# A recurrent feature encoder on one core: first digits ahead, halves of h exchanged by DMA, the wide cell half a round sooner, and a dense layer that reads h in place

## The reference, cut to what matters

```python
def lstm_last(x, Wx, Wh, b):          # x: [B, T, E]
    def step(carry, xt):
        h, c = carry
        i, f, gg, o = jnp.split(xt @ Wx + h @ Wh + b, 4, axis=-1)
        c = sigmoid(f) * c + sigmoid(i) * tanh(gg)
        h = sigmoid(o) * tanh(c)
        return (h, c), None
...
m_from = lstm_last(base_emb[from_seq], seq_Wx, seq_Wh, seq_b)    # T = 64, H = 64
m_to = lstm_last(base_emb[to_seq], seq_Wx, seq_Wh, seq_b)
...
x = concatenate([ne[nums], fe[fr]], axis=-1)                     # 11 features, T = 32, E = 8, H = 8
nwf = vmap(enc)(...)
...
feats = concatenate([goby, is_indel, matches_ref, m_from, m_to, count_fwd, count_rev, nwf], axis=-1)
return relu(feats @ reduce_W + reduce_b)                         # [2048, 64]
```

## Time and profile before

| | |
|---|---|
| median of 3 runs | 1803.08 us (1800.8 to 1803.32) |
| the profiled execution | 1799.57 us |
| its span, first to last instruction | 1797.7 us |
| TensorE (PE) busy | 1680.6 us, 93% |
| VectorE (DVE) busy | 1462.9 us, 81% |
| ScalarE (ACT) busy | 1464.5 us, 81% |
| GpSimd (POOL) busy | 944.8 us, 53% |
| mean granted TensorE clock | 0.987 of full speed |
| read from HBM | 474.17 MB |

### The profile page before, as it was taken

One profiled execution on the slowest core, in us unless ns is written; L12 is line 12 of the kernel. 1 busy time (PEld: TensorE's weight loads), 2 busy tenths in 40 slices (PEclk: granted clock), 3 DMA queues, 4 the chain that ended last, 5 costly groups with the idle time before them and its releaser, 6 DMA issues.

```text
span 1797.7 us, 59515 instructions
## 1 busy us (share of the span) xinstructions
PE 1680.6 (93%) x24900; PEld 765.0 (43%) x24900; DVE 1462.9 (81%) x1443; ACT 1464.5 (81%) x2531; POOL 944.8 (53%) x478
## 2 busy tenths in 40 slices
PE   2789999999999999999999999999999999999995
PEld 0234444444444444444444444444444444444444
DVE  6768888888888888988888888888888888888771
ACT  1468888888888888888888888888888888888883
POOL 5346666666666666444444444444554444444552
PEclk9899999999999999999999999999999999999997
DMA  6868898999988988889898888989888888888832
GB/s 224 299 223 261 281 290 285 275 289 277 293 279 284 286 284 285 276 270 298 277 284 289 275 277 278 290 277 285 280 286 279 282 272 296 283 277 282 282 119 49
DMA packets 153476, 484.37 MB, mean 269 GB/s; under 512 B 39240, under 2 KB 95096, under 8 KB 108024
## 3 DMA queue, kind: packets, MB, share of 16 engines
q1 hardware_dynamic: 149532, 479.52, 82.5%
q0 software_dynamic: 2560, 0.15, 0.5%
q10 hardware_dynamic: 1116, 0.88, 0.1%
HBM read 474.17 MB, written 6.09 MB: 267 GB/s over the span
## 4 chain that ended last, share of the span: by engine, by line
PE 64%; ACT 18%; POOL 7%; issue 6%; DMA 1%; SPq 0%; DVE 0%; ACTq 0%; POOLq 0%
PE ab L515 28%; PE e_ps L438 15%; PE f_ps L515 10%; ACT gate L555 10%; PE ab L465 7%; POOL nwf_h L612 4%; ACT tanh_c L555 4%; POOL ig L585 4%; PE ab L401 3%; ACT seq_x L408 2%; ACT f_ps L564 1%; ACT gate L564 1%; ACT nwf_x L478 1%; DMA last_h<-nwf_h 0%; PE e_ps L828 0%
## 5 line engine op out<-in xcount | busy, mean ns | idle before, releaser
L585 POOL TENSOR_TENSOR ig<-gate 128x1024 f32<-128x1024 f32 x192 | 411.1, 2141 | 810.1 <-ACT seq_x L408 404.2
L428 DVE TENSOR_SCALAR hot<-low,cst 128x4096 bf16<-128x4096 bf16 x352 | 453.4, 1288 | 152.8 <-PE e_ps L438 149.4
L438 PE MATMUL e_ps<-hot,tab 128*32 128x512 bf16 x8448 | 527.2, 384 | 15.9 <-DVE kept L450 15.9
L450 DVE SCALAR_TENSOR_TENSOR kept<-high,cst,e_ps 128x1024 f32<-128x1024 uint8 x352 | 448.8, 1275 | 32.9 <-PE e_ps L438 22.1
L515 PE MATMUL ab<-seq_h,seq_wh 64*64 64x512 f32 x3072 | 411.0, 593 | 0.0
L438 PEld LDWEIGHTS e_ps<-hot,tab 128*32 128x32 bf16 x8448 | 204.3, 97 | 399.0 <-issue 228.9
L612 POOL TENSOR_TENSOR seq_h<-gate,tanh_c 128x1024 f32<-128x1024 f32 x128 | 303.9, 2374 | 1.4 <-ACT tanh_c L555 1.4
L562 ACT ACTIVATE gate<-ab 128x1024 f32<-128x1024 f32 x256 | 263.2, 1028 | 18.2 <-PE ab L515 15.0
L555 ACT ACTIVATE tanh_c<-seq_c 64x512 f32<-64x512 f32 (+1 forms) x384 | 241.9, 630 | 25.3 <-POOL nwf_h L612 22.2
L555 ACT ACTIVATE gate<-ab 64x512 f32<-64x512 f32 (+1 forms) x384 | 228.3, 595 | 11.5
L564 ACT ACTIVATE gate<-ab,nwf_bias 128x256 f32<-128x256 f32 (+1 forms) x384 | 147.4, 456 | 104.0 <-PE ab L515 99.9
(11 more groups left out here) (67 smaller groups left out, 1608.5 us busy)
## 6 DMA issues: line engine op xcount, KB each, us to landing
low<-low_digits SPq DMA_DIRECT2D x352, 1024.0 KB, 8.0
tok<-seq_tokens SPq DMA_DIRECT2D x128, 384.0 KB, 4.9
high<-high_digits SPq DMA_DIRECT2D x1408, 32.0 KB
raw<-in_indices SPq DMA_DIRECT2D x32, 176.0 KB
low_digits<-low_of SPq DMA_DIRECT2D x32, 88.0 KB, 3.0
high_digits<-high_of SPq DMA_DIRECT2D x32, 44.0 KB, 3.6
gate<-in_tokens SPq DMA_DIRECT2D x1, 1024.0 KB, 5.7
low<-last_h SPq DMA_DIRECT2D x11, 64.0 KB
```

What stands on the lines that cost most here:

```text
L428: nc.vector.tensor_scalar(hot[:, p % HOT_RING, :, :, :].rearrange("p g u c -> p (g u c)"), low[:, p % LOW_RING, :, :].rearrange("p u c -> ...
L438: last = nc.tensor.matmul(e_ps[32 * g:32 * g + 32, i, :], tab[:, part, 2 * m + ty, :], hot[:, p % HOT_RING, g, i, :], start=(part == 0), s ...
L450: nc.vector.scalar_tensor_tensor(out=kept[:, p % KEPT_RING, :, :].rearrange("p u c -> p (u c)"), in0=high[:, p % HIGH_RING, :, :].rearrang ...
L585: nc.gpsimd.tensor_tensor(ig[:, cols], gates[0][:, n % 2, cols], gates[1][:, n % 2, cols], ALU.mult).then_inc(ig_ready, 1)
```

## The change

- `CELLS`: the wide nwf cell of step r stands at the end of round r, and the narrow cell of step r - 1 behind the first two seq cells. The list ends with the narrow cell alone.
- The shares of pairs are 2, 2, 1, 2, 2, 2 (in the first round 2, 2, 2, 2, 3).
- nwf gate 3 and tanh of c are made in place (fewer, wider pieces), so block 1 of h has its halves swapped; SP's queue issues two DMAs (`move_q`) for each nwf cell that put them right into a second tile `nwf_hq`, from which the next step's products read block 1. The products and the new h wait for `q_moved`.
- Step 0 of each cell leaves out the product with h, and h is no longer set to zero.
- The start: the indices of round 0 and their digits come first; tokens are loaded, stored and broadcast by the ACT queue; the digits of round 1 are made in cell 0, those of round 2 in cell 3; the few indices in cell 1; the small weights are placed by VectorE in cells 2 and 3; the gathers begin in cell 8. In cells 1 to 4, GpSimd makes the last cell's h ahead of the input product.
- The end: no transfer through DRAM. The weights of the 88 small dimensions are loaded once a row and spread by a mask over four slots (`place_dense_w`), and 44 products of 32 rows by 256 columns read the last h as it lies; four more take the small embeddings.

```diff
-for _r in range(NWF_T + 1):
-    for _p in range(2):
-        if _r < NWF_T:
-            CELLS += [("seq", 2 * _r + _p, 0), ("seq", 2 * _r + _p, 1)]
-        if _r:
-            CELLS.append(("nwf", _r - 1, _p))
+for _r in range(NWF_T):
+    CELLS += [("seq", 2 * _r, 0), ("seq", 2 * _r, 1)]
+    if _r:
+        CELLS.append(("nwf", _r - 1, 1))
+    CELLS += [("seq", 2 * _r + 1, 0), ("seq", 2 * _r + 1, 1), ("nwf", _r, 0)]
+CELLS.append(("nwf", NWF_T - 1, 1))
...
-    _share = [3, 3, 3, 2] if _r == 0 else [2, 2, 2, 2, 2, 1]
+    _share = [2, 2, 2, 2, 3] if _r == 0 else [2, 2, 1, 2, 2, 2]
...
-FIRST_ROUNDS = 2
-ROUND_AT = {(2 if _r == 2 else NUMBER["nwf", _r - 3, 1]): _r for _r in range(FIRST_ROUNDS, NWF_T)}
+FIRST_ROUNDS = 1
+ROUND_AT = {(0, 3)[_r - 1] if _r < 3 else NUMBER["nwf", _r - 3, 1]: _r for _r in range(FIRST_ROUNDS, NWF_T)}
...
                     at_least(pe, h_ready, NUMBER[kind, step - 1, k] + 1)
+                    if kind == "nwf":
+                        pe.wait_ge(q_moved[k], 32 * step)
...
             def h_rhs(rows, block, a, b):
+                if kind == "nwf" and block:
+                    return nwf_hq[k][rows, a:b]
...
-            last = at_h(to, of, pieces(n, g), GATES[g][1]) if g == 3 else in_place(to, of, n, g)
+            if g == 3 and CELLS[n][0] == "seq":
+                last = at_h(to, of, pieces(n, g), GATES[g][1])
+            else:
+                last = in_place(to, of, n, g)
...
+        def move_q(sp, n):
+            _, step, k = CELLS[n]
+            wp, wq = widths(n)
+            sp.wait_ge(h_ready, n + 1)
+            for half in range(2):
+                sp.dma_start(nwf_hq[k][64 * half:64 * half + 64, :], nwf_h[k][64 - 64 * half:128 - 64 * half, wp:wp + wq]
+                             ).then_inc(q_moved[k], 16)
...
+        def dense_nwf(pe, k):
+            pe.wait_ge(h_ready, NUMBER["nwf", NWF_T - 1, k] + 1)
             (pat, wp, _), (qat, wq, _) = PARTS[k]
+            for block, at, w, a in ((0, pat, wp, 0), (1, qat, wq, wp)):
+                pe.wait_ge(dense_step, 2 * k + block + 1)
+                for j in range(w // LANES):
+                    for r in range(4):
+                        rows = slice(32 * r, 32 * r + 32)
+                        last = nc.tensor.matmul(sums_of(r ^ (2 * block)), nwf_h[k][rows, a + j * LANES:a + (j + 1) * LANES],
+                                                dense_w[rows, at // LANES + j, :, :].rearrange("p s o -> p (s o)"),
...
@@ @block.sync
-                sp.dma_start(few_in, few).then_inc(s_few, 16)
-                sp.dma_start(tok_raw, tokens).then_inc(s_tokens, 16)
-                for r in range(FIRST_ROUNDS):
+                for r in range(2):
                     load_raw(sp, r)
...
                 store_digits(sp, 0)
...
+                for p in range(LOW_RING):
                     load_pair(sp, p)
+                sp.dma_start(few_in[:, :, :], few).then_inc(s_few, 16)
+                load_raw(sp, 2)
...
+                    if n >= 2 and CELLS[n - 2][0] == "nwf" and CELLS[n - 2][1] + 1 < NWF_T:
+                        move_q(sp, n - 2)
...
@@ @block.vector
-                make_few(dve)
+                make_digits(dve, 0)
                 make_tokens(dve)
-                make_digits(dve, 0)
                 make_x_weights(dve)
                 make_tables(dve)
-                make_digits(dve, 1)
...
+                    if n == 1:
+                        make_few(dve)
+                        dve.wait_ge(s_rows, 16)
+                    elif n in (2, 3):
+                        place_nwf_w(dve, n - 2)
```

More of the change, by code:

```diff
@@ L130, in build @@
 def build(nc, few, tokens, indices, goby_emb, bool_emb, count_emb, tables, seq_x_w, seq_h_w, rows, bias, rest_rows,
-          seq_rows, consts, out):
+          seq_rows, dense_rows, consts, out):
     ctx = ExitStack()
@@ L263, in build @@
         h_ready = sem("h_ready")
+        q_moved = [sem(f"q_moved{k}") for k in range(2)]
         state_set = sem("state_set")
         nwf_w_ready = sem("nwf_w_ready")
-        h_in_dram = [sem(f"h_in_dram{c}") for c in range(2)]
-        rest_here = sem("rest_here")
-        y_summed = sem("y_summed")
+        dense_here = sem("dense_here")
+        dense_ready = sem("dense_ready")
+        dense_step = sem("dense_step")
+        small_w_ready = sem("small_w_ready")
         y_ready = sem("y_ready")
@@ L524, in gate @@
                 every = ((0, CH), (0, CH))
-                tiles(lambda rows, half, block: seq_wx[rows, place, :],
-                      lambda rows, block, a, b: x[rows, block, a:b], every, True, False)
-                last = tiles(lambda rows, half, block: seq_wh[rows, place, :], h_rhs, every, False, True)
+                last = tiles(lambda rows, half, block: seq_wx[rows, place, :],
+                             lambda rows, block, a, b: x[rows, block, a:b], every, True, not step)
+                if step:
+                    last = tiles(lambda rows, half, block: seq_wh[rows, place, :], h_rhs, every, False, True)
             else:
@@ L531, in gate @@
                     spans = [s and (s[1], s[1] + s[2]) for s in sets]
-                    tiles(lambda rows, half, block: nwf_w[rows, 1 - half, sets[block][0], place, :],
-                          lambda rows, block, a, b: x[rows, PARTS[k][block][0] + a:PARTS[k][block][0] + b],
-                          spans, True, False)
-                    last = tiles(lambda rows, half, block: nwf_w[rows, half, sets[block][0], place, :],
-                                 h_rhs, spans, False, True)
+                    last = tiles(lambda rows, half, block: nwf_w[rows, 1 - half, sets[block][0], place, :],
+                                 lambda rows, block, a, b: x[rows, PARTS[k][block][0] + a:PARTS[k][block][0] + b],
+                                 spans, True, not step)
+                    if step:
+                        last = tiles(lambda rows, half, block: nwf_w[rows, half, sets[block][0], place, :],
+                                     h_rhs, spans, False, True)
             last.then_inc(f_ready if g == FORGET else ab_ready, 1)
@@ new lines, in place_small_w, with sums_of @@
+        def place_small_w(dve):
+            dve.wait_ge(s_late, 32)
+            nc.vector.tensor_tensor(small_w[:, :, :], rest_w[:, None, :].to_broadcast([P, 4, OUT]),
+                                    cst[:, C_QUARTER:C_QUARTER + 4, None].to_broadcast([P, 4, OUT]),
+                                    ALU.mult).then_inc(small_w_ready, 1)
+        def sums_of(quad):
+            bank = e_ps if quad < 2 else ab[USE["dense"] % 2]
+            return bank[:, quad % 2, 0:4 * OUT]
+        def dense_nwf(pe, k):
+            pe.wait_ge(h_ready, NUMBER["nwf", NWF_T - 1, k] + 1)
+            (pat, wp, _), (qat, wq, _) = PARTS[k]
+            for block, at, w, a in ((0, pat, wp, 0), (1, qat, wq, wp)):
[5 more added lines that the diff above has]
+                                                dense_w[rows, at // LANES + j, :, :].rearrange("p s o -> p (s o)"),
+                                                start=False, stop=(k == 1 and block == 1 and j == w // LANES - 1),
+                                                skip_group_check=True)
+                last.then_inc(dense_step, 1)
@@ L752, in _ @@
             def _(act):
-                for dst, src, there in ((cst[:, :], consts, s_cst), (xb_f, seq_x_w, s_x_w),
+                for dst, src, there in ((tok_raw, tokens, s_tokens), (cst[:, :], consts, s_cst), (xb_f, seq_x_w, s_x_w),
                                         (tab_f, tables, s_tables), (seq_wh[:, :, :], seq_h_w, s_h_w),
-                                        (nwf_rows[:, :, :, :], rows, s_rows), (nwf_bias[:, :, :], bias, s_bias),
-                                        (rest_w[:, :], rest_rows, s_late), (seq_out_w[:, :], seq_rows, s_late)):
+                                        (nwf_rows[:, :, :, :], rows, s_rows), (nwf_bias[:, :, :], bias, s_bias)):
                     act.dma_start(dst, src).then_inc(there, 16)
+                act.wait_ge(tokens_made, 1)
+                act.dma_start(tok_dram.rearrange("t (k h) z o l -> (t k) (h z o l)", k=2), tok_of
+                              ).then_inc(tokens_stored, 16)
+                for s in range(AHEAD):
+                    load_tokens(act, s)
                 for s in range(AHEAD):
```

143 lines of the change are left out of this document (72 added, 71 removed).

## The result

The changed kernel takes **1772.45 us** (median of 4 runs, 1770.14 to 1777.11) against 1803.2 before (1800.8 to 1805.72): ratio 0.9833, 95% interval 0.9808 to 0.9857, so 30 us less. The profiled execution has a span of 1771.0 us where before it was 1797.7. I forecast 1768, with 1763.0 for the span.

The account below looks back on a forecast made before the run. TensorE was taken to bound the rounds. Start 83 + 31 rounds x 53.42 + tail 24 gave a 1763.0 us span, 34.7 less than before, so a median of 1768 us; range 1745 to 1792.

Parts of the forecast that it names:

- The three waits that go: TensorE's waits behind the wide cell, behind the narrow cell and before its gates vanish: together 1.02 us less a round.
- 51.88 us of TensorE work: The old round of 52.90 us less its 1.02 us idle, taken as TensorE's work in each round.
- The new stall of 1.19 us: In the wide cell, the second set's sum waits for ScalarE to empty gate 3's bank: 1.19 us a round.
- The new stall of 0.35 us: In the cell without a sum, TensorE's second lookup waits for VectorE's `kept` product to free `e_ps`: 0.35 us a round.
- The exchange at nothing: The DMAs moving halves of h, 320 KB a round on SP's queue, were priced at no added time.
- The start, 83: From the span's start to the end of cell 4, the first wide cell: 83 us, bounds 76 and 98.
- VectorE is in command: From first `kept` at 29 us to the first wide cell's end, VectorE's work sets the pace: 52.7 us.
- The start bound by transfers: Rival: pair loads come no faster at the start, so cell 4 ends at 98 and the total is 1783; chance 0.15.
- The tail, 24: From T, the end of the last wide cell's gates, to the span's end: 24 us against 36 before.
- T + 27: Tail if 32-row weight loads take as long as 128-row ones, counted from the last wide gates: total 3 us more.
- The clock: Rival: a grown stall drops TensorE's clock from 2.4 to 1.2 GHz each round, giving 1815 us; chance 0.07.
- did collide: Against the rival that the wide cell's two sums don't collide: round 51.88 us, total 1720; chance 0.09.

Follow-up runs that it names:

- the sum moved: In the wide cell, TensorE makes the second set's sum behind the first lookup instead of ahead of it, against the changed kernel: 1745.91 us, ratio 0.9689 to the kernel before.
- the even shares: Lookup pairs shared 2, 2, 2, 2, 1, 2 over a round's cells, so every cell sums one set, against the changed kernel: 1756.57 us, ratio 0.9759 to the kernel before.
- six buffers with the sum moved: Six buffers for the high digits instead of five, on the kernel with the second sum behind the first lookup: 1738.31 us, ratio 0.9669 to the kernel before.

## Why the prediction was right

The sum was 83 + 31 x 53.42 + 24 = 1763.0 us of span; the trace has 93.6 + 31 x 53.37 + 22.9 = 1771.0. Of the 8.0 us missed, the start is 10.6, the rounds -1.5 and the tail -1.1. Of the 26.7 us of span gained, the start gave 28.2 where I had 39 (the span before less 31 rounds of 52.90 and the tail of 36 is 121.8, against 93.6), the tail 13.1, and the rounds took 14.6, where the sum had 16. This counts the old rounds at 52.90; some of them were longer too (up to 54.42), and in the mean, from the 128-column sum at 154.58 to that at 1745.11, they were 53.02. By that mean the start gave 24.5 and the rounds took 10.9.

- **The three waits that go** (0.49, 0.37, 0.16): right. None is in the trace. Undoing the exchange brings back 0.50 behind the wide cell's gate 3, and 0.29 behind the narrow cell's, now at the next large cell's gate 1; its 0.15 is a new one, at a token lookup. The 0.16 goes with the order of the cells, as I had it: it stays with the old order. There a round is 51.71, 1.19 less than before, with 0.86 (0.49 and 0.37) of idle gone. So the idle numbers under-read by 0.33 us, and "51.88 us of TensorE work" was too high by as much.
- **The new stall of 1.19 us**: right. The trace calls it 1.03, and taking it away shortened a round by 1.21 to 1.25.
- **The new stall of 0.35 us**: right, 0.34 in the timeline. It also stays with the sum moved; the even shares took it, and it isn't in the round shown of the kernel without the exchange.
- **The exchange at nothing**: right for TensorE's waits. Its transfers weren't tried alone.
- **Not in the sum**: 0.45 us a round while the gathers run, some 14 rounds, 6 us; and some rounds of up to 55.1. They filled what the work term had too much. An undisturbed round without gathers is 53.0, so that 53.42 fits the mean of 53.37 this well is luck.
- **The start, 83**: the failed step. "I put TensorE's first gate at 24" gave 29.31, and from first `kept` to the end of cell 4 I had 54 us where 61 passed. Of the first 5.3, 4.0 are the pair loads under way beside the tokens' hops (25.29 when two of them wait). I had used the faster digits for the loads and left out that the loads now compete with the tokens. The first `kept` then followed in 3.4 us, not 5. For the second 7 the step that failed is "VectorE is in command": from 32.75 to 93.6 it was busy for 51.35 us of 60.85, where the sum had it busy throughout; its waits are 5.3 us behind TensorE's lookups, 3.2 behind GpSimd's products and 2.4 without a releaser. Some 4 us of its busy time are an excess of two small operations, one of the few indices and one of the digits, which took 2.24 and 2.37 us beside a GpSimd product where their like take 0.17 and 0.25. The weight placements aren't shown to be among the causes: placing them early gave 3.8 us, and the sum had 3.7 for them. What each wait cost wasn't tried.
- **The start bound by transfers** (the rival): half right. Sharing cost the first gate 4 us, but removing it alone gave nothing, and cell 4 ended at 93.6, not 98.
- **The tail, 24**: right at 22.9, last h at T + 11.2 for 11.3. The dense layer behind the 16 products (4 + 44) ran from 1758.69 to 1767.0, 8.3 us for 8.5. The 44 of 32 rows (two passes each, 88 in the trace) took 6.2 of these, in row groups side by side. The rule of the Trainium skill, page "TensorE: Matmul & The Clock Gate", section "LDWEIGHTS (loading the stationary operand)", that a 32-row load takes as long as a 128-row one, holds for one load, which the trace has at 0.18 us with 32 rows and at 0.19 with 128 (loads by form from 1755 to 1768 us):

```profile
L687 PEld LDWEIGHTS e_ps<-low,nwf_h 32*128 32x128 f32 x44 | 4.1, 184 | 1.1 <-issue 1.1
L878 PEld LDWEIGHTS ab<-seq_out_w,seq_h 128*128 128x128 f32 x16 | 1.9, 192 | 0.0
```

  The pace that I drew from it for the tail, T + 27, doesn't hold, since 88 such loads were through in 6.2 us, 0.07 each: they run beside each other.
- **The clock**: right. 1.00 in the window of rounds with 1.03 us idle in each; it was not pushed to where it falls. The sums **did collide**, as said.

## What to carry to other kernels

Price an engine's freed time only up to the next wait: here the exchange was worth 1.2 us a round in the old order and 0.7 in the new, and the new order took 1.3 back by putting two sums into one cell, most of which moving one sum on TensorE repaired. When the bound engine gets faster, look at the DMA share in the same windows: at 0.92 this kernel still ran evenly, at 0.94 to 0.99 executions of one kernel differed by 9 to 48 us, and further gains were partly lost. An operation moved to another engine costs its own time there, and a small one can cost ten times that where it meets a GpSimd product; a load issued earlier costs what it does to the transfer that decides.

## What the hardware showed that I had not expected

- GpSimd's 128 x 1024 product took 6.57 us beside a VectorE product of 128 x 1536 and two compares, 3.71 us beside compares, and mostly 2.37 elsewhere; VectorE's addition of 16 columns (the few indices) took 2.24 us beside such a product, where its neighbours took 0.17, and one digit operation 2.37 instead of 0.25:

```profile
44.94 2.24 DVE L323 TENSOR_TENSOR few_f<-few_f,few_idx 128x16 f32<-128x16 f32 x1
...
69.32 2.37 DVE L322 TENSOR_SCALAR wrap<-near 128x352 int16<-128x352 int16 x1
```

  In each case the sizes say that the one stood until the other was done: the 6.57 are 2.37 and the 4.2 us from 57.17 to the end of the second compare (61.31); the two small operations end within 0.2 us of the product that began at 44.78 and at 69.20 and took 2.37. The Trainium skill, page "GPSIMD Engine Reference", section "1. Specifications", says that GpSimd's way to SBUF is shared with VectorE and contends with its two-input instructions and those of a two-port mode; the trace agrees, and gives the price: 1.3 to 4.2 us for one GpSimd product, 2.1 for one small operation of VectorE. In which mode a VectorE instruction runs, no row shows.
- In one execution (cells in the old order) the DMA engines moved 293 GB/s at a share of 0.98 and 278 at 1.03. The share alone doesn't give the rate: at the start of the kernel before, 1.04 went with 322 GB/s.
- The spread between executions went with the DMA share from 100 to 1700 us: 2 us at 0.76, 5 at 0.86 (the exchange undone), 7 and 6 at 0.92 (the changed kernel, and six buffers with the sum moved), 20 at 0.94, 9, 21 and 28 at 0.95 (three kernels), 48 at 0.99. The share is that of the profiled execution alone and rises in a burst, so this doesn't say which of the two makes the other.
- One gather in each cell, issued by an engine that is idle for half of the time, lengthened a round by 0.45 us with the shares 2, 2, 1, 2, 2, 2, and by nothing in the kernel before, with even shares or in the old order.
